# Two-stage residual kernel on Trainium2: five raw products with W instead of six, the bias of every group's third product added on VectorE from `b_raw`, and a new order at the start

## The reference

```python
# x: (64, 128, 512); per sequence: a mask type in 0..2 and a category in 0..63
attn_in = jnp.tanh(jnp.einsum('bsd,da->bsa', hidden, W1) + b1)       # A = 128
scores  = jnp.einsum('bsa,a->bs', attn_in, v)
mask    = prefix (l <= j), postfix (l >= j) or cloze (l != j), by type
p       = softmax(where(mask, scores[:, None, :], NEG_INF))
pooled  = jnp.einsum('bjl,bld->bjd', p, hidden) / cnt[..., None]
x = x + pooled
x = x + jnp.einsum('bsd,bdh->bsh', x, W[cat_ids]) + b[cat_ids][:, None, :]
```

## Time and profile before

| | us |
|---|---|
| median of 3 runs | 308.31 |
| lowest, highest | 308.03, 309.88 |
| the profiled execution | 308.65 |
| its span in the trace | 306.9 |
| granted clock of PE, share of full | 0.999 |

### The profile page before, as it was taken

The page is one execution under the profiler, slowest core; times in us unless marked ns, Lnnn a source line. Parts: engine busy times, 40 slices in busy tenths (PEclk is TensorE's granted clock), DMA queues, the critical chain, the costliest instruction groups (busy, mean ns, idle before and its releaser), DMA issues.

```text
span 306.9 us, 4890 instructions
## 1 busy us (share of the span) xinstructions
PE 301.0 (98%) x1284; PEld 233.0 (76%) x1284; DVE 278.0 (91%) x385; ACT 262.6 (86%) x429; POOL 85.6 (28%) x119
## 2 busy tenths in 40 slices
PE   8999999999999999999999999999999999999995
PEld 4445488788887878878787887878788787888884
DVE  4447998999999999999999999999999999999961
ACT  2265889989899998999999899999989999898942
POOL 5120302224341233425223341421434132202000
PEclk9999999999999999999999999999999999999999
DMA  7999999999999999899999999999999999986133
GB/s 264 412 388 414 390 400 398 373 418 356 392 347 359 386 314 420 305 395 355 378 366 309 413 351 360 358 344 386 331 407 347 357 378 326 402 315 219 70 136 137
DMA packets 23516, 105.69 MB, mean 344 GB/s; under 512 B 2625, under 2 KB 2626, under 8 KB 13378
## 3 DMA queue, kind: packets, MB, share of 16 engines
q1 hardware_dynamic: 23058, 103.03, 89.2%
q10 hardware_dynamic: 432, 2.36, 1.9%
HBM read 88.61 MB, written 16.78 MB: 343 GB/s over the span
## 4 chain that ended last, share of the span: by engine, by line
PE 88%; issue 5%; DMA 2%; DVE 2%; POOLq 1%; ACT 1%; POOL 1%; ACTq 0%
PE ps_y L682 17%; PE ps_y L684 17%; PE ps_y L683 17%; PE ps_pre L641 13%; PE ps_y L694 5%; PE ps_y L695 5%; PE ps_y L696 5%; PE ps_y L700 4%; PE ps_pT L658 2%; DMA w_raw<-in_L_cond_W 2%; PE ps_y L670 1%; PE ps_scores L651 1%; PE ps_scores L649 1%; DVE w_lo L484 1%; POOLq L293 1%
## 5 line engine op out<-in xcount | busy, mean ns | idle before, releaser
L484 DVE TENSOR_TENSOR w_lo<-w_raw,w_hi 128x2048 fp32r<-128x2048 f32 x58 | 134.9, 2326 | 0.0
L351 ACT ACTIVATE w_hi<-w_raw 128x2048 fp32r<-128x2048 f32 x58 | 111.7, 1927 | 9.1 <-POOL w_raw L287 7.4
L682 PE MATMUL ps_y<-w_hi,xT_hi 128*128 128x512 f32 x232 | 91.7, 395 | 0.0
L684 PE MATMUL ps_y<-w_hi,xT_lo 128*128 128x512 f32 x232 | 90.5, 390 | 0.0
L683 PE MATMUL ps_y<-w_lo,xT_hi 128*128 128x512 f32 x232 | 90.3, 389 | 0.0
L287 POOL TENSOR_TENSOR w_raw<-w_raw,ident 128x512 f32<-128x512 f32 x26 | 33.6, 1294 | 113.0 <-DVE w_lo L484 74.5
L684 PEld LDWEIGHTS ps_y<-w_hi,xT_lo 128*128 128x128 f32 x232 | 43.5, 188 | 9.4
L683 PEld LDWEIGHTS ps_y<-w_lo,xT_hi 128*128 128x128 f32 x232 | 43.6, 188 | 8.8
L682 PEld LDWEIGHTS ps_y<-w_hi,xT_hi 128*128 128x128 f32 x232 | 43.6, 188 | 8.6
L512 DVE TENSOR_TENSOR z_lo<-ps_y,z_hi 128x512 fp32r<-128x512 f32 x64 | 43.6, 682 | 7.2 <-ACT z_hi L387 7.2
L387 ACT ACTIVATE z_hi<-ps_y 128x512 fp32r<-128x512 f32 x64 | 38.8, 606 | 9.7 <-PE ps_y L684 5.1
(11 more groups left out here) (70 smaller groups left out, 363.5 us busy)
## 6 DMA issues: line engine op xcount, KB each, us to landing
w_raw<-in_L_cond_W SPq DMA_DIRECT2D x62, 1024.0 KB, 8.4
out<-out_sb SPq DMA_DIRECT2D x64, 256.0 KB, 6.0
x_raw<-in_x SPq DMA_DIRECT2D x15, 1024.0 KB, 7.0
out_sb<-in_L_cond_b SPq DMA_DIRECT2D x16, 256.0 KB, 5.4
w_raw<-in_L_cond_W ACTq DMA_DIRECT2D x2, 1024.0 KB, 6.3
x_raw<-in_x SPq DMA_DIRECT2D x2, 512.0 KB, 4.8
w_pack<-in_W_b_v ACTq DMA_DIRECT2D x1, 257.0 KB, 2.8
b_raw<-in_L_cond_b SPq DMA_DIRECT2D x2, 128.0 KB, 8.7
```

The source lines that it names most:

```text
L351: nc.scalar.activation(w_hi[k % NH][:], w_raw[k % NW][:], ACT.Copy).then_inc(w_hi_ready, 1)
L484: nc.vector.tensor_tensor(w_lo[k % NL][:], w_raw[k % NW][:], w_hi[k % NH][:].bitcast(F32), ALU.subtract).then_inc(w_lo_ready, 1)
L682: nc.tensor.matmul(y[:], xT_hi[q][:, c, xs], w_hi[k % NH][:, c, :], start=(c == 0), stop=False)
L684: last = nc.tensor.matmul(y[:], xT_lo[q][:, c, xs], w_hi[k % NH][:, c, :], start=False, stop=(c == DC - 1))
```

## The change

- RAW goes from 6 to 5: the product with W of sequence 5 is a split one, its W is split, and the columns of x of sequence 5 are split with those of 6 and 7.
- WIDE goes from 1 to 2, and only from group 2 on (FIRST_WIDE): sequences 10, 14, ... 62 have their bias added on DVE, 14 in all for 16. Sequences 1 and 5 now get the fourth product and a copy by ACT.
- The bias row is loaded into `b_raw`, once `b_both` is made and the wide sum before has read it, one turn earlier (b = 1 for b = 2), and not at the start of the program. The wait for the store that last used `out_sb[2]` is on DVE in `add_wide`; SP has none for it.
- `add_wide(g-1)` stands in the turn with b = 1 for b = 0, in each case three turns after its product; the last one stands after the loop.
- The lists of ACT and DVE for the start are in another order.

```diff
-    WIDE = 1
+    WIDE = 2
+    FIRST_WIDE = 2
...
-    RAW = 6
+    RAW = 5
...
         def wide(k):
-            return k % G == WIDE
+            return k % G == WIDE and k >= G * FIRST_WIDE
+
+        def copied(k):
+
+            return sum(not wide(i) for i in range(k + 1))
...
             if wide(k):
-                engine.wait_ge(sum_ready, k // G + 1)
+                engine.wait_ge(sum_ready, k // G - FIRST_WIDE + 1)
             else:
-                engine.wait_ge(out_ready, k - (k + G - WIDE - 1) // G + 1)
+                engine.wait_ge(out_ready, copied(k))
...
             def load_wide(g):
                 cat = load_cat(G * g + WIDE)
-                if g >= 1:
-                    sp.wait_ge(out_stored[WIDE], 16 * g)
-                sp.dma_start(out_sb[WIDE][:], bias[bass.ds(cat, 1), :].to_broadcast([P, D])).then_inc(wide_in, 16)
+                if g == FIRST_WIDE:
+                    sp.wait_ge(bias_ready, 2)
+                else:
+                    sp.wait_ge(sum_ready, g - FIRST_WIDE)
+                sp.dma_start(b_raw[:], bias[bass.ds(cat, 1), :].to_broadcast([P, D])).then_inc(wide_in, 16)
...
             load_w(6)
-            load_wide(0)
...
-                if b == 2 and 1 <= g < GROUPS:
+                if b == 1 and FIRST_WIDE <= g < GROUPS:
                     load_wide(g)
...
             tanh_group(1)
+            split_w_hi(5)
             split_xT_hi(2)
+            split_z_hi(3)
+            copy_out(0)
             exp_group(1)
+            copy_out(1)
             split_w_hi(6)
-            copy_out(0)
-            split_z_hi(3)
+            scale_group(1)
             split_w_hi(7)
             split_z_hi(4)
-            scale_group(1)
+            split_mix_hi(1)
             split_w_hi(8)
             split_z_hi(5)
-            split_mix_hi(1)
+            tanh_group(2)
             copy_out(2)
-            tanh_group(2)
             split_w_hi(9)
+            copy_out(3)
             split_z_hi(6)
-            copy_out(3)
+            copy_out(4)
+            exp_group(2)
             split_w_hi(10)
-            exp_group(2)
-            copy_out(4)
...
                 dve.wait_ge(pz_done, k + 1)
-                dve.wait_ge(wide_in, 16 * (g + 1))
-                nc.vector.tensor_tensor(out_sb[WIDE][:], ps_y[k % NY][:], out_sb[WIDE][:], ALU.add)\
+                dve.wait_ge(wide_in, 16 * (g - FIRST_WIDE + 1))
+                dve.wait_ge(out_stored[WIDE], 16 * g)
+                nc.vector.tensor_tensor(out_sb[WIDE][:], ps_y[k % NY][:], b_raw[:], ALU.add)\
                     .then_inc(sum_ready, 1)
...
             split_mix_lo(0)
+            split_z_lo(2)
             split_xT_lo(1)
             add_identity(4)
...
-            split_z_lo(2)
+            add_identity(5)
             split_av_lo(1)
-            add_identity(5)
             max_group(1)
+            split_w_lo(5)
             add_identity(6)
             split_xT_lo(2)
             row_scale_group(1)
-            add_wide(0)
+            split_z_lo(3)
             add_identity(7)
             split_w_lo(6)
-            split_z_lo(3)
             add_identity(8)
             split_w_lo(7)
             split_z_lo(4)
-            split_w_lo(8)
             add_identity(9)
+            split_z_lo(5)
             split_mix_lo(1)
             split_av_lo(2)
-            split_z_lo(5)
+            split_w_lo(8)
+            max_group(2)
             add_identity(10)
-            max_group(2)
+            add_identity(11)
             split_w_lo(9)
+            row_scale_group(2)
             split_z_lo(6)
-            add_identity(11)
-            row_scale_group(2)
...
                 split_z_lo(k - 1)
-                if b == 0:
+                if b == 1 and g - 1 >= FIRST_WIDE:
                     add_wide(g - 1)
...
+            add_wide(GROUPS - 1)
```

## The result

The changed kernel takes 306.48 us (median of 22 runs, 305.82 to 308.79); the kernel before, over 22 runs of the same calls, 308.41. The ratio is 0.994, with a 95% interval of 0.9921 to 0.9959: 1.3 to 2.4 us less, a small gain that is clear of noise. The profiled execution took 307.15 us, 0.67 above the median, with a span of 305.4.

A forecast was written before the change was run, and what follows sets the result against it. DVE was taken to bind by a hair, from scores to `xT_lo`, in an 18.13 us loop with PE (17.99 alone). Place -1.3 and start +0.2 gave -1.1: 308.65 to 307.5 profiled, median 307.2; range 305.5 to 309.3.

The forecast's parts named there:

- What bounds the kernel now: Even stretch: a loop through DVE and PE sets the 18.13 us period; PE alone would need 17.99.
- Part 1, the place: Wide sum moved behind `xT_lo`: DVE-PE loop falls from 18.13 to 17.53 us, saving 1.3 us over 12 groups.
- two ties: Loops through ACT and DVE near PE's 17.99 us cost some jitter, so 0.11 of 0.14 us per group is gained.
- The POOL step: On DVE, `w_lo` no longer meets POOL's identity sum and gets 0.20 us back, 2.48 to 2.28.
- the loop through it: Even stretch: the loop from POOL's sum through ACT's `w_hi` and DVE back to POOL takes 17.98 us.
- Part 2, banks and transfers: PSUM banks, the wide sum's store and the loads queued behind it: W leaves 3.5 us later but in time; cost 0.
- this cover: SP's queue: the load of W behind the wide sum's store lands with 0.6 us to spare before DVE's identity sum.
- Parts 3 and 4, the start: PE could reach group 3's `hidden` 1.8 us earlier, but DVE's wait for W11 puts it at 58.9 against 58.71.
- the term "+0.2": Net effect of the start on the time: +0.2 us, from -0.9 to +0.9.
- "The start pays too": Rival: at the start W11 lands near 48 and PE's gaps vanish; -3.0 us, 305.3; chance 0.15.
- "Nothing comes of the place": Rival: in the even stretch DVE alone closes its loop at 18.05 to 18.13 us; about 308.0; chance 0.22.
- "slower by ACT's copy": Rival: ACT's new copy makes `w_hi` late, loop 18.18 to 18.4 us; +1.0, 309.5; chance 0.15.

The follow-up runs named there:

- e3_old_place: Changed kernel with WIDE = 1 and the wide sum back one turn earlier, ahead of `xT_lo`; 308.59 us, ratio 0.9989.
- e5: Changed kernel plus one DVE step per group right ahead of the wide sum, 448 columns of the same sum into a spare tile; 313.91 us, ratio 1.0160.
- e6: Changed kernel with POOL's identity sum of the sequences with b = 1 started one DVE step later, after `z_lo`; 317.95 us, ratio 1.0280.
- e9_changed_again: The changed kernel run again without an edit; 306.83 us, ratio 0.9954.
- e7_raw6_new_lists: Changed kernel with six raw products again, new start lists kept, `w_hi(5)` and `w_lo(5)` taken out; 307.03 us, ratio 0.9946.
- e2: Kernel before with five raw products and the new start lists, its wide sums kept as they were; 310.35 us, ratio 1.0042.
- e12: e1 with five raw products for six, `w_hi(5)` and `w_lo(5)` put into the old start lists; 308.14 us, ratio 0.9979.
- e1: Changed kernel with the old start, six raw products and the old lists with one edit each, so the wide part alone; 306.36 us, ratio 0.9924.
- e10: e1 run again without an edit; 305.96 us, ratio 0.9932.
- e11_pool_takes_10: Changed kernel with W 11's identity sum at its old place at the start and W 10's on POOL; 306.61 us, ratio 0.9920.

## Why the prediction was right

**What bounds the kernel now.** Right. Not PE alone but DVE's stretch from the scores to `xT_lo` and PE's from `hidden` to the scores set the period. e3_old_place shows it: 18.13 comes back with the sum's old place alone, and 0.14 us of PE with it.

**Part 1, the place.** Right in kind, a little low in size: I took 0.11 of the 0.14 us for jitter of two ties, and 0.127 came (1.52 / 12). The POOL step was right, `w_lo` 2.48 to 2.27; the ends of ACT's `w_hi` (94.24 for 94.21) and the length of the loop through it (17.98) were right, as e5 and e6 show by adding to it. What I missed: `xT_lo`, 0.60 earlier, now meets the end of POOL's mask copies and loses 0.10. It cost nothing, for that loop stood at 17.53 + 0.10, still under PE's 17.99. I had not seen it because it takes two steps: the identity sum, 0.60 earlier, lies beside POOL's last copy, which takes longer, and the end of that copy then lies beside `xT_lo`.

**Part 2, banks and transfers.** Right for the profiled execution. The load of W for product 4g + 8 left SP at 82.92, 16.95 us after the scores at 65.97, for 16.8 forecast, and landed 6.6 later, 1.9 ahead of its identity sum at 91.41; DVE never waits for a load from 62 us on. That this cover is thin shows in other executions of the same code: DVE waited for this load once in e9_changed_again (0.15) and once in e7_raw6_new_lists (1.00). DMA is no bound of the period: the same bytes per group now pass in 18.00 us. The Trainium skill (SBUF — State Buffer, "A bandwidth-pool intuition that's wrong") gives some 358 GB/s between HBM and a core. From 62 to 280 us this kernel moved 360, reads and stores together, and that was no limit here: the period could shrink, and the stretch of the earlier trace rows moved 401.

**Parts 3 and 4, the start.** The forecast of 58.9 for `hidden` of group 3, by W 11 landing at 49.6, met the first profile to 0.05 us (58.85, 49.6), and PE's stall ahead of `pz(6)` came too, if shorter (0.45 us for the 1.2 I had). That agreement is partly luck: PE's first raw product started 0.9 later in this execution than in the profile that I had stepped from. Counted from that product, group 3 comes after 48.84 us before and 48.08 in the changed kernel, so the start gained 0.8 where I had forecast a loss of 0.2. The step took one execution's loads for the kernel's. In e9_changed_again, the same code with PE starting as early as before (9.88), W 11 lands at 48.1, there is no such wait, and group 3 comes at 57.57, 1.1 earlier than before. Over many runs the start gave more than the +0.2 of the sum: the medians differ by 1.93 us, of which the even stretch gives 1.5 in the profiles. So the term "+0.2" is the one that was mis-sized, by 0.6 us or so, and that is most of the 0.7 by which the forecast of 307.2 was high; the place's 1.5 for 1.3 is the rest. What I had right is that one raw product less brings no time at the start: counted from the first raw product, the changed kernel (48.08, 47.69) is no faster to group 3 than the wide part alone with six raw products (47.85, 47.67). That DVE has no room for it fits e2 and e12, but no run shows it by itself.

**Why the start gained at all** is seen from e1 and e10: two wide sums less on DVE before group 3, 1.2 us, let PE run without a gap. By starts, PE's two stalls of the earlier trace rows had cost 0.56 and 0.90 us; the two bias products on PE cost 0.46. That leaves 1.0, and e1's 47.85 for 48.84 is that. That is from the wide part (FIRST_WIDE = 2), not from five raw products or new lists. The prediction booked those 1.2 us to pay for `w_lo(5)`, and in the changed kernel they do.

**The rivals.** "The start pays too" did not come as the median, but e9's profiled execution is close to it: W 11 at 48.1, no stall ahead of `pz(6)`, 305.95 us for its 305.3. "Nothing comes of the place" and "slower by ACT's copy" fell with the period of 18.00, the latter by 0.02 us of room (17.98 for 18.00): e5 shows that its mechanism stands right behind.

**The best version.** Nothing that ran is clearly below the changed kernel. e1_wide_only's ratio was about 0.2% below the changed kernel's both times, within the intervals, with a smaller edit; e11_pool_takes_10 has the lowest ratio. What would settle a difference of 0.2% is more runs than these.

## What to carry to other kernels

When two engines hand work to each other once per round, neither's busy share tells the bound; find the loop, add its stretches, and ask of each step whether it stands inside the binding stretch or outside. Moving 0.60 us of work past the hand-over was worth 0.13 us a round here without any work removed, and the rest of the 0.60 only made another loop of the same length visible. And read the landing times of the first loads from more than one execution before a step of the start is costed by them.

## What the runs showed of the hardware that I had not expected

The size of the hold between DVE and POOL is regular. A DVE subtraction of two SBUF tiles that starts while POOL's operation runs took longer by the rest of POOL's time less some 0.12 us: 0.82 for 0.94 (e6_pool_late), 0.20 for 0.33, 0.10 for 0.23 (`xT_lo` and the mask copies, after), and 0.15 for 0.27 (the `w_lo` at 48.46 behind POOL's sum, e11_pool_takes_10). The other way round POOL's sum took 2.53 us for 1.30 beside a `w_lo` that had begun first (the same run). DVE steps with one input in PSUM, `z_lo` at 0.68 us and the wide sum, show none of it beside the same POOL sum. The Trainium skill (SBUF — State Buffer, "Who interferes with whom") calls this an exclusive lock held for a whole instruction, and the traces agree, but for those 0.12 us.

PE's first raw product started anywhere from 9.85 to 10.88 us in these executions, by when the first x and W landed. That, and the wait for W 11, can be the whole difference between two executions of one kernel: the two profiled ones of the changed kernel took 307.15 and 305.95 us, 1.20 apart, and were 1.28 apart at `hidden` of group 3.
